# A transformer layer with cross attention and experts: scores of two heads in the row halves of TensorE, from float32r parts, and a new order in the step

## The reference

```python
# x, ctx: (4, 512, 256); 16 heads of 16 columns
q = split_heads(layernorm(x) @ Wq.T + bq)
k = split_heads(ctx @ Wk.T + bk)
v = split_heads(ctx @ Wv.T + bv)
attn = softmax(einsum('bhqd,bhkd->bhqk', q, k) / 4, axis=-1)
x = x + tanh(g_xattn) * (merge_heads(attn @ v) @ Wo.T + bo)
h = layernorm(x)
# 2 of 8 experts a token (silu-gated, 256 wide), and a shared gated product (512 wide)
x = x + tanh(g_ffn) * (experts(h, top2(h @ w_router)) + (silu(h @ gate_w) * (h @ up_w)) @ down_w)
```

## Time and profile before

| | us |
|---|---|
| median of 3 runs (459.63 to 461.47) | 459.9 |
| span of the profiled execution | 466.8 |
| TensorE, VectorE, ScalarE busy in it | 453.6, 331.8, 252.6 |

### The profile page before, as it was taken

One profiled execution on the slowest core, in us unless ns is written; L12 is line 12 of the kernel. 1 busy time (PEld: TensorE's weight loads), 2 busy tenths in 40 slices (PEclk: granted clock), 3 DMA queues, 4 the chain that ended last, 5 costly groups with the idle time before them and its releaser, 6 DMA issues.

```text
span 466.8 us, 8100 instructions
## 1 busy us (share of the span) xinstructions
PE 453.6 (97%) x2310; PEld 215.8 (46%) x2310; DVE 331.8 (71%) x841; ACT 252.6 (54%) x540; POOL 154.4 (33%) x209
## 2 busy tenths in 40 slices
PE   8999999999999999999999989889999999999997
PEld 8664432222222222222465634565555555555745
DVE  1988898888888888888578766354565656532674
ACT  2664477777777777777565111023666766631110
POOL 5493488111212121212132766600323332332000
PEclk9999999999999999999999999979999999999999
DMA  8669762335353535353548522311322222312921
GB/s 261 223 181 251 157 204 58 86 83 97 90 98 94 98 94 97 95 92 102 167 135 264 211 91 81 110 48 46 93 84 88 85 88 83 90 49 60 377 101 47
DMA packets 54140, 56.71 MB, mean 121 GB/s; under 512 B 13456, under 2 KB 44560, under 8 KB 54096
## 3 DMA queue, kind: packets, MB, share of 16 engines
q1 hardware_dynamic: 47504, 43.82, 34.1%
q0 software_dynamic: 4960, 10.53, 7.4%
q10 hardware_dynamic: 1632, 1.84, 1.2%
HBM read 36.35 MB, written 17.72 MB: 116 GB/s over the span
## 4 chain that ended last, share of the span: by engine, by line
PE 90%; DVE 4%; issue 2%; DMA 1%; SPq 1%; another core or an unknown queue 1%; POOL 1%; ACT 1%; DVEq 0%; POOLq 0%
PE PS L1395 13%; PE PS L1305 13%; PE PS L1523 12%; PE PS L1567 11%; PE PS L1677 9%; PE PS L1580 6%; PE PS L1696 5%; PE PS L1357 4%; PE PS L1672 3%; PE PS L1442 3%; PE PS L1691 2%; PE PS L1651 2%; DVE nmax L842 2%; PE PS L1335 2%; PE PS L1659 2%
## 5 line engine op out<-in xcount | busy, mean ns | idle before, releaser
L842 DVE TENSOR_REDUCE nmax<-PS 128x1 f32<-128x512 f32 x256 | 159.4, 683 | 21.4 <-PE PS L1305 21.4
L730 ACT ACTIVATE R<-PS 128x512 f32<-128x512 f32 x256 | 134.1, 601 | 42.0 <-PE PS L1523 41.7
L1305 PE MATMUL PS<-R 96*128 96x512 bf16 x256 | 96.1, 382 | 1.2 <-DMA R<-k_parts 1.0
L1523 PE MATMUL PS<-R 98*128 98x512 bf16 x256 | 86.2, 380 | 0.3 <-DVE R L860 0.3
L1395 PE MATMUL PS<-R 128*32 128x512 f32 x512 | 68.2, 604 | 0.0
L621 POOL DMA_INDIRECT token_y<-R,dest x34 | 32.6, 960 | 93.4 <-DVE R L1184 92.0
L1305 PEld LDWEIGHTS PS<-R 96*128 96x128 bf16 x256 | 24.8, 97 | 69.7 <-DVE nmax L842 51.1
L1677 PE MATMUL PS<-R 128*128 x100 | 47.3, 595 | 0.2 <-ACT R L798 0.2
L745 ACT ACTIVATE R<-PS 128x512 f32<-128x512 f32 x16 | 9.6, 597 | 68.7 <-PE PS L1567 52.1
L600 POOL DMA_DIRECT2D CH<-R x56 | 27.4, 496 | 54.4 <-ACT R L718 54.4
L1523 PEld LDWEIGHTS PS<-R 98*128 98x128 bf16 x256 | 24.8, 97 | 38.6 <-ACT R L730 22.6
(11 more groups left out here) (177 smaller groups left out, 598.4 us busy)
## 6 DMA issues: line engine op xcount, KB each, us to landing
R<-q_parts SPq DMA_DIRECT2D x96, 64.0 KB, 3.1
R<-k_parts SPq DMA_DIRECT2D x96, 64.0 KB, 3.1
R<-in_fc_w_dram SPq DMA_DIRECT2D x16, 256.0 KB
R<-token_y SPq DMA_DIRECT2D x4, 1024.0 KB, 9.0
R<-slot_x SPq DMA_DIRECT2D x25, 129.0 KB
k_parts<-R SPq DMA_DIRECT2D x8, 384.0 KB, 3.3
q_parts<-R SPq DMA_DIRECT2D x8, 384.0 KB, 3.5
fc<-in_fc_w_dram SPq DMA_DIRECT2D x16, 128.0 KB
```

Of the source, the lines that this page charges most:

```text
L730: nc.scalar.activation(PT[:, kt, j, :], PS[:, (G * (TB * i + kt) + j) % 3, :], ACT.Exp).then_inc(exp_done, 1)
L842: nc.vector.tensor_reduce(nmax[:, i % 2, j * TB + qt:j * TB + qt + 1], PS[:, smax_bank(n), :], AX.X, ALU.max, negate=True).then_inc(max_re ...
L1305: mm(PS[:, smax_bank(n), :], QS[g][0:KS, j, qt * P:(qt + 1) * P], KST[g][0:KS, j, :], start=True, stop=True).then_inc(smax_done, 1)
L1523: mm(PS[:, n % 3, :], KST[g][0:KM, j, kt * P:(kt + 1) * P], QS[g][0:KM, j, :], start=True, stop=True).then_inc(st_done, 1)
```

## The change

q and k are split into two float32r parts: `first_part` writes the high one, `rest` the low one straight into `QP`. `REST`, `second_part` and `third_part` are gone, and the DRAM copies are f32. `TERMS` is 3, so a head's product has 48 rows, 50 with the maxima, and heads 2h and 2h + 1 of a group stand at partitions 0 and 64 of the same columns (`HALF`); their matmuls use the array's upper and lower 64 rows. `QK` is a float32r name for the memory of `R1`. A group's loads are again twelve, of 64 KB. GpSimd fills all of `KST` with ones before the loads.

The maxima are ordered so that n even and odd are the two heads of a pair. In the loop VectorE reduces two adjacent banks by one instruction (`two_max`), from banks 4 to 7 in turn; 28 tiles come early instead of 24. `split_max` on VectorE splits the 16 maxima columns into two parts before they are turned, `max_transpose` turns both at once at the head of step three (kt = 2), into a bank of the three score banks, where they take a turn between the scores (`score_turn`, `max_turn`, `turn_free`); `max_rows` on ScalarE copies them, and `load_max` waits once. All four scores and both pairs of maxima now stand ahead of the values, and the copy of the outputs follows the first exponential of the second step. Values go to bank 3, the banks of the tail are 4 to 6, and `bias_row` comes before the loop.

```diff
-    TERMS = 6
-    Q_PART = [0, 1, 2, 0, 1, 0]
-    K_PART = [0, 0, 0, 1, 1, 2]
+    TERMS = 3
+    Q_PART = [0, 1, 0]
+    K_PART = [0, 0, 1]
+    UNIT = 2 * TERMS
+    HALF = P // 2
...
+        with nc.sbuf_tensor("QK", [P, 8192], F32R) as QK:
+            pass
         R1 = sb("R1", [P, 8192])
...
+        QS = [QK[:, 1024 * g:1024 * (g + 1)].rearrange("p (h n) -> p h n", h=2) for g in range(NG)]
+        KST = [QK[:, 4096 + 1024 * g:4096 + 1024 * (g + 1)].rearrange("p (h n) -> p h n", h=2) for g in range(NG)]
...
-        EARLY = 6 * G
-        EARLY_J = ((0, 0, 0, 0), (0, 0, 0, 0), (2, 2, 2, 2), (2, 2, 2, 2))
+        EARLY = 7 * G
+        EARLY_J = ((0, 0, 0, 0), (0, 0, 0, 0), (2, 2, 2, 2), (2, 2, 4, 4))
...
+        MT_AT = 2 * G + 2
+        def score_turn(i, kt, j):
+            return (G * TB + 1) * i + G * kt + j + (i + 1 < GROUPS and G * kt + j >= MT_AT)
+        def max_turn(i):
+            return (G * TB + 1) * (i - 1) + MT_AT
...
             def load_max(i):
-                for part, s in ((0, m1_ready), (1, m2_ready)):
-                    sp.wait_ge(s, i + 1)
+                sp.wait_ge(m_ready, i + 1)
+                for part in range(2):
...
-            def third_part(b, j):
-                pool.wait_ge(q2_ready, 4 * b + j + 1)
-                nc.gpsimd.tensor_tensor(QP[:, j, 2, :], REST[:, j, :], QP[:, j, 1, :], ALU.subtract).then_inc(q3_ready, 1)
...
-            def second_part(b, j):
-                act.wait_ge(rest_ready, 4 * b + j + 1)
-                nc.scalar.copy(QP[:, j, 1, :], REST[:, j, :]).then_inc(q2_ready, 1)
...
-                nc.scalar.copy(mparts[:, i % 2, 0, :], PS[0:G * TB, 7, 0:P]).then_inc(m1_ready, 1)
+                nc.scalar.copy(mparts[:, i % 2, :], PS[0:2 * G * TB, max_turn(i) % 3 if i else 7, 0:P]).then_inc(m_ready, 1)
...
-                        if j == 2 and kt == 0 and i:
+                        if j == 0 and kt == 1 and i:
                             out_copy(i - 1)
-                        if j == 1 and kt == 2 and i + 1 < GROUPS:
-                            m_first(i + 1)
+                        if G * kt + j + 1 == MT_AT and i + 1 < GROUPS:
+                            max_rows(i + 1)
...
+            def two_max(n):
+                i, _, at = max_tile(n)
+                for r in range(2):
+                    dve.wait_ge(smax_done[r], n // 2 + 1)
+                nc.vector.tensor_reduce(nmax[:, i % 2, at:G * TB:G * TB // 2], PS[:, smax_bank(n):smax_bank(n) + 2, :], AX.X,
+                                        ALU.max, negate=True).then_inc(max_ready, 1)
+            def split_max(i):
+                dve.wait_ge(max_ready, maxima(G * TB * (i + 1)))
+                if i >= 2:
+                    dve.wait_ge(mt_done, i - 1)
+                nc.vector.tensor_copy(nmax_parts[:, i % 2, 0, :].bitcast(F32R), nmax[:, i % 2, :]).then_inc(high_max, 1)
+                dve.wait_ge(high_max, i + 1)
+                nc.vector.tensor_tensor(nmax_parts[:, i % 2, 1, :], nmax[:, i % 2, :], nmax_parts[:, i % 2, 0, :],
+                                        ALU.subtract).then_inc(split_ready, 1)
...
+            def turn_free(turn):
+                i, m = divmod(turn - 3, G * TB + 1)
+                if turn < 3:
+                    return
+                if i + 1 < GROUPS and m == MT_AT:
+                    pe.wait_ge(m_ready, i + 2)
+                else:
+                    pe.wait_ge(exp_done, G * TB * i + m - (i + 1 < GROUPS and m > MT_AT) + 1)
...
-                    mm(PS[:, n % 3, :], KST[g][0:KM, j, kt * P:(kt + 1) * P], QS[g][0:KM, j, :],
-                       start=True, stop=True).then_inc(st_done, 1)
+                    turn = score_turn(i, kt, j)
+                    turn_free(turn)
+                    h, r = divmod(j, 2)
+                    at = slice(HALF * r, HALF * r + KM)
+                    mm(PS[:, turn % 3, :], KST[g][at, h, kt * P:(kt + 1) * P], QS[g][at, h, :],
+                       start=True, stop=True).then_inc(st_done[r], 1)
...
                     scores(kt, 0)
                     scores(kt, 1)
-                    mx[0]()
-                    scores(kt, 2)
-                    mx[1]()
                     if kt == 2 and i + 1 < GROUPS:
                         max_transpose(i + 1)
+                    mx[0]()
+                    mx[1]()
+                    scores(kt, 2)
+                    mx[2]()
+                    mx[3]()
+                    scores(kt, 3)
                     if kt:
                         values(i, kt - 1)
...
-                    mx[2]()
-                    scores(kt, 3)
-                    mx[3]()
                     tail(TB * i + kt - TAIL)
```

More of the change, by code:

```diff
@@ L10 @@
 F32 = mybir.dt.float32
-BF16 = mybir.dt.bfloat16
+F32R = mybir.dt.float32r
 U32 = mybir.dt.uint32
@@ L204, in flamingo_layer @@
         wq_scaled = sem("wq_scaled")
-        q1_ready, q2_ready, q3_ready = (sem(n) for n in ("q1_ready", "q2_ready", "q3_ready"))
-        rest_ready = sem("rest_ready")
+        high_ready, low_ready = sem("high_ready"), sem("low_ready")
         qp_out = sems("qp_out", 4)
@@ L403, in _ @@
                 if 0 < i and i + 3 < GROUPS:
-                    load_group(i + 3, range(0, TERMS - 2))
+                    load_group(i + 3, range(0, UNIT - 2))
                 if i + 1 < GROUPS:
@@ L407, in _ @@
                 if 0 < i and i + 3 < GROUPS:
-                    load_group(i + 3, range(TERMS - 2, TERMS))
+                    load_group(i + 3, range(UNIT - 2, UNIT))
                 if 0 <= i - 1 < TURNED:
@@ L717, in out_copy @@
                     act.wait_ge(ot_t, i - TURNED - 1)
-                nc.scalar.copy(OT[i % 2], PS[:, 6, :]).then_inc(ot_ready, 1)
+                nc.scalar.copy(OT[i % 2], PS[:, 3, :]).then_inc(ot_ready, 1)
             def h2t_first(b):
@@ L893, in _ @@
                 for j in range(4):
-                    if b == B - 1 and j == 2:
-                        m_second(0)
+                    if b == B - 1 and j == 1:
+                        split_max(0)
                     early_max(EARLY_J[b][j])
@@ L898, in _ @@
             early_max(EARLY - sum(map(sum, EARLY_V + EARLY_J)))
-            def head_max(s):
-                for qt in range(TB):
-                    one_max(TB * s + qt)
             def scale_of(i):
@@ L953, in h2t_second @@
                 dve.wait_ge(h2_t, 2 * b + 2)
-                dve.wait_ge(st_done, G * TB * (GROUPS - 1 + b // 2))
+                for r in range(2):
+                    dve.wait_ge(st_done[r], G // 2 * TB * (GROUPS - 1 + b // 2))
                 nc.vector.tensor_copy(H2T[:, 1, b * S:(b + 1) * S], PS[:, bank("h2_t", b, 1), :]).then_inc(h2t_ready[1], 1)
@@ L1118, in _ @@
             dve.wait_ge(consts, 9)
+            bias_row()
             for i in range(GROUPS):
                 for kt in range(TB):
-                    s = smax_schedule(i, kt)
-                    if i == 0 and kt == 1:
-                        bias_row()
-                    for qt in range(TB):
-                        if s is not None:
-                            one_max(TB * s + qt)
-                        n = TB * kt + qt - OUT_AT
-                        if n == 0 and 0 <= i - 2 < TURNED:
+                    t = smax_schedule(i, kt)
+                    for h in range(2):
+                        if t is not None:
+                            two_max(TB * t + 2 * h)
+                        if kt == 0 and h == 1 and i + 1 < GROUPS:
+                            split_max(i + 1)
+                        if kt == 1 and h == 0 and 0 <= i - 2 < TURNED:
                             scale_of(i - 2)
-                        if n == 0 and i > TURNED:
+                        if kt == 1 and h == 0 and i > TURNED:
                             denominators(i - 1)
-                        if n == 1 and i > TURNED:
+                        if kt == 1 and h == 1 and i > TURNED:
                             head_out(i - 1)
-                        if TB * kt + qt == M2_AT and i + 1 < GROUPS:
-                            m_second(i + 1)
                     tail(TB * i + kt - TAIL)
@@ L1285, in scores_for_max @@
             def scores_for_max(n):
[L1287 to L1288 removed]
+                i, (h, r, qt), _ = max_tile(n)
                 b, g = divmod(i, NG)
[L1290 to L1291 removed]
+                if n % (G * TB) == 0:
+                    pe.wait_ge(ld_group[g], 16 * 2 * UNIT * (b + 1))
+                at = slice(HALF * r, HALF * r + KS)
                 if n == 0:
@@ L1400, in out_transpose @@
                 pe.wait_ge(ot_ready, i + 1)
-                pe.wait_ge(m2_ready, min(i + 2, GROUPS))
+                pe.wait_ge(max_ready, maxima(G * TB * GROUPS))
                 wait(pe, ctx_ready, i - TURNED)
@@ L1411, in bank_free @@
                 if n < 3:
-                    pe.wait_ge(max_ready, G * TB * GROUPS)
+                    pe.wait_ge(max_ready, maxima(G * TB * GROUPS))
                     return
@@ L1482, in bias_product @@
```

(4 more changed lines are left out.)

175 lines of the change are left out of this document (78 added, 97 removed).

## The result

| median of 4 runs | us |
|---|---|
| before | 460.69 (459.63 to 461.72) |
| after | 466.45 (465.82 to 466.93) |
| ratio | 1.0127, 95% interval 1.0085 to 1.0169 |

The changed kernel is slower by 1.3%. The forecast was faster by 1%, so the sign is wrong; the time lies just inside the range. The profiled execution of after took 466.15 us, with a span of 464.4. The profiled one of before that the prediction used was of a slower execution, whose excess lies behind 252 us; for a comparison by stages I profiled the same kernel again (459.54 us, span 457.8, clock 1.00).

A forecast was written before the change was run, and what follows sets the result against it. The prediction took TensorE to bound the kernel. Thirteen groups -9.1, group zero's last step -0.2, group fourteen -0.5, front +1.4 and last six steps +3.9 summed to -4.5, so 455.4 us; range 443 to 467.

The forecast's parts named there:

- float32r in one pass: Loop's score and maxima matmuls: a float32r slot of 512 columns takes 0.22 us, as in bf16.
- the halves side by side: Loop's scores and maxima: two heads run together in the array's halves, five slots instead of eight, 1.10 us instead of 1.76.
- hidden loads: TensorE's float32r weight loads: 0.11 us into an idle array, nothing where a matmul of 0.22 us runs.
- a loop of waits of 2.55 us: Loop step: fourth score waits for the first exponential, values behind it; 2.55 us sets the step, 0.29 less than before.
- loads that don't hide: Rival for the row halves: 0.33 us a matmul, group 11.5, no gain, total about 465 us; chance 0.13.
- the rival of the late rows: Rival: maxima rows reach the next group late, half a microsecond a group, 461 us; chance 0.07.
- the loop's links: Waits between engines in a loop step: 0.42, 0.60, 0.03, 0.11, 0.31, 1.00 and 0.08, sum 2.55 us; group 10.8.
- the price of the array's division: Maxima visits among full-array matmuls in the front: each changes the division twice, about +0.5 us together.
- VectorE's part in the front: Before the loop: four more maxima (4 x 0.60) and the bias row end the first step about 1.9 us later.
- the fourth rival: Maxima rows come late for the next group, half a microsecond a group, 461 us; chance 0.07.
- Only the two single visits pay: about +0.5: Front: a pair of maxima saves 0.22 against edges of 0.24, so only two single visits cost time, about +0.5 us.
- +3.9: Last six steps: +0.58 us each from the loop of waits, and 0.4 for the ring of score banks' extra turn.

The follow-up runs named there:

- one_half: The changed kernel with both heads of a pair read from the lower row half; 632.23 us.
- values_fourth: The changed kernel with values put back between the third score and the second pair of maxima; 483.22 us, ratio 1.0541.
- half_visits: The kernel before, with its 24 early maxima matmuls reading only 48 rows; 462.83 us, ratio 1.0082.
- before_again: The kernel before, unchanged and profiled once more; 459.54 us, span 457.8.
- tail_order: The changed kernel with the fourth score behind values again in the last six steps; 465.55 us, ratio 1.0128.
- front_pairs: The changed kernel with early maxima always two a visit and the last four tiles right before the loop; 467.19 us, ratio 1.0189.
- filled: The changed kernel with nine small full-array matmuls of ones between the last early maxima and in the first two steps; 465.06 us, ratio 1.0115.
- half_tail: The kernel before, with score matmuls in the last six steps reading only 48 rows; 460.53 us, ratio 1.0028.
- tuned: filled with tail_order's tail and the copy of the outputs one step earlier in the last group; 462.10 us, ratio 1.0083 against the kernel before.

## Why the prediction was wrong

**Right.** float32r in one pass, the halves side by side (the first maxima start 0.34 after the two scores do, load included, not 0.46), hidden loads, and a loop of waits of 2.55 us, measured 2.61. The second step of a group is 2.75 instead of 2.60, for the copy of the outputs, which values wait for, ends 1.61 us into the step (183.78 plus 0.58) and not 1.49; the third 3.09 as against 3.10, in part by luck, for the 0.06 of the links stands where the 0.05 of a late start was forecast and didn't come; the two-bank reduction 1215 ns (1.12 us estimated); VectorE 9.70 us a group, as forecast, and not the bound. The Trainium skill ("TensorE: Matmul & The Clock Gate", Part 3, The mechanism) has a load overlap a running matmul only in another row group; here the trace disagrees: in one_half the load of 0.33 us vanished in a slot of 0.43 of the same half.

That 466.45 lies inside the range is luck. Its upper end stood there for loads that don't hide, and they did hide. Two small sums of the prediction are off by its own numbers: the last step of group zero gains 0.29, not 0.2, and the rival of the late rows comes out at 462, not 461.

No one step turned the sign. Four were wrong in size or missing: the loop's links, the price of the array's division, VectorE's part in the front, and the clock.

**The loop: right mechanism, size too good.** A group takes 11.06 us, not 10.8: 0.06 from the links in each of two steps (with the load's 0.08 counted into the first link, no one of them is off by over 0.04), and 0.15 in the second step. Over the fourteen distances between transposes that is 3.6 us of the missing gain. Two groups were longer, 11.84 and 11.64 us, because the maxima rows came 0.72 and 0.51 late (at 146.97 and 213.91 us): the fourth rival, twice in fourteen instead of each time.

**A premise was wrong, though no term rested on it.** "That makes a loop of waits that the old order doesn't have" is false: values_fourth shows it at 2.85 us, and the kernel before runs just at it. Traced in both kernels, it shows what the new order does: it takes two maxima matmuls (0.44) out of the loop, and the wider loads put some 0.2 back. The narrower matmuls without the new order give nothing: values_fourth has 12.54 us a group against 11.50.

**The front: the division and four more tiles.** "Only the two single visits pay: about +0.5" was the step that failed. It priced the change of the array's division as if its edges cost what they do beside the values, and a pair's saving paid for them. half_visits measured 3.35 us for such visits. In after the pairs do run side by side, and its own trace gives the price there, visit by visit against before_again. Lines of after:

```profile
56.67 0.50 PE L1320 MATMUL PS<-QK 48*128 48x512 f32 x2
...
59.02 0.73 PE L1320 MATMUL PS<-QK 48*128 48x512 f32 x3
60.30 0.49 PE L1320 MATMUL PS<-QK 48*128 48x512 f32 x1 [0.55 <-DVE nmax L851]
...
62.63 0.73 PE L1320 MATMUL PS<-QK 48*128 48x512 f32 x3
```

and of before_again:

```profile
56.36 0.60 PE L1305 MATMUL PS<-R 96*128 96x512 bf16 x2
...
58.51 0.60 PE L1305 MATMUL PS<-R 96*128 96x512 bf16 x2
```

A visit of two and its four matmuls take 2.35 us (56.67 to 59.02) instead of 2.15; a single visit and its four 1.50 (46.45 to 47.95) instead of 1.09. Over all visits that is about 2.7 us, where 0.5 was forecast. A visit of four takes 3.61 (59.02 to 62.63) instead of 2.15, so besides the 0.2 the two more tiles and TensorE's wait for VectorE cost 1.26, twice: 2.5. (The profile's wait of 0.55 is only the part that no earlier record covers.) The turning of the maxima, with its wait of 0.41, costs 0.6 more. That is 3.1 in place of the 1.9 that I had for VectorE's part. The first tile came only 0.3 earlier than in before_again, not 1.0 (in tail_order 1.6). 2.7 + 3.1 - 0.3 = 5.5. front_pairs gets 0.2 of it back, so it is not a matter of where the four tiles stand.

**The clock in group zero: not among the steps or rivals.** Narrow pairs with waits between them follow the start-up there, and the granted clock is 0.56 from 71 to 77 us. filled shows its price, 1.7 us. In this execution only this place has it: over the groups behind it the same matmuls have 1.00.

**The last six steps: the waits right, the division left out.** +3.9 was for waits and nothing for the division; +5.4 was measured. The second of the six steps in after:

```profile
237.07 0.73 PE L1548 MATMUL PS<-QK 50*128 50x512 f32 x3
238.26 0.49 PE L1548 MATMUL PS<-QK 50*128 50x512 f32 x1 [0.45 <-ACT R L742]
```

From its first score to its projection (239.68) it is 2.61 us, where before_again has 1.96 for the same matmuls: +0.65 instead of +0.58. Over the six steps this part, the waits, is 4.5 longer, against 3.9. The rest is 0.9: the projection's eight instructions take 1.92 until the next scores instead of 1.73, as in half_tail. half_tail's whole 1.6 doesn't apply, for there a score stands right before each projection, and in after values do. tail_order and tuned get 1.0 and 2.4 of the 5.4 back.

**Sum of the misses:** loop and group zero 6.7 (3.6 for the links, 1.9 for the clock by 12.94 against 11.06, 1.4 for the late rows, and -0.2 by roundings), front 4.1 (2.2 for the division, 1.2 for VectorE and the four tiles, 0.7 for the load), last steps 1.5 (0.9 and 0.6), and -1.1 behind the loop, where nothing was changed: 11.2, against the 11.1 between -4.5 and +6.6.

**Left open:** why filled's clock fell in the last steps in its profiled execution; and whether a fourth score bank would open the loop of waits, which wasn't tried, since all eight banks are in use.

## What to carry to other kernels

Trace the loop of waits through the banks (score, its exponential, the score that gets its bank, what stands behind that one) in the old kernel as well as in the new. Where its length equals the engine's own work, taking work away from the engine gains only if the loop gets shorter too. Price the edges with the same care as the steady part: here the loop gained 4.5 us in thirteen groups, and 28 early tiles, group zero and six late steps, through the array's division, the clock and their waits, lost more than twice that. Two edits that each lose alone (+1.3 and +1.0 us a group) can gain together (-0.4), so a part that was measured alone says little of the whole.

## What the runs showed of the hardware

- A visit of two matmuls over 48 rows between full-array f32 matmuls costs 0.3 us more than one over 96 rows (2.45 against 2.15 us); 24 tiles in the front cost 3.35 us from the first tile on, and six steps with two visits each 1.6. With float32r pairs side by side in two halves a visit costs 0.2 more (2.35). The Trainium skill ("TensorEngine Tiling (Array Packing)", Key Properties) says that a change of tiling mode drains the array. The trace agrees in that each change costs time, and these are the prices here; the drain itself no run shows.
- With its narrow matmuls in one half alone TensorE had the lower clock for a whole group (granted 0.50); with pairs in both halves it had 1.00 in the steady loop and 0.56 in a part of group zero, where waits stand between them; nine small full-array matmuls in such waits kept it at 1.00 there (filled). The kernel before had 1.00 in both.
- A float32r matmul of 512 columns over 48 rows, alone or as a pair in two halves, gives way to the next in 0.23 us, with a weight load of 0.19 us, where the bf16 load takes 0.10.
